# A graph network on one core: six of a basis' sixteen pieces mixed in the bucket stage, and deeper rings of one-hots in the placing stage

## The reference

```python
def rgcn_gate_layer(x, row, col, edge_type, basis, att, gate_w, root, bias):
    w = jnp.einsum('rb,bio->rio', att, basis)      # 30 bases of 512 x 512 mixed into 2 relations
    x_j = x[col]
    msgs = []
    for r in range(2):
        gate = jax.nn.sigmoid(x_j @ gate_w[r, :, 0])
        msgs.append(gate[:, None] * x_j @ w[r])
    msg = jnp.where((edge_type == 0)[:, None], msgs[0], msgs[1])
    return jax.ops.segment_sum(msg, row, num_segments=1250) + x @ root + bias
...
x = _layernorm(x + _L0_gnn_ref(x, edge_index_t, 1250, L0_gnn_W, L0_gnn_b), axis=-1)
...
x = _layernorm(x + _L3_gnn_ref(...), axis=-1)
```

## Time and profile before

| | |
|---|---|
| median of 3 runs | 1955.77 us (1955.05 to 1958.15) |
| profiled execution: time, and span of its instructions | 1963.35 us, 1961.5 us |
| bucket stage, first VectorE instruction to that of the next stage | 138.00 to 182.68 us |
| placing stage, likewise | 182.68 to 314.61 us |
| busy over the span: TensorE, its weight loads, VectorE, ScalarE, GpSimd | 82%, 50%, 59%, 24%, 35% |

### The profile page before, as it was taken

How to read it: one execution, slowest core, us unless ns; L and a number is a source line. 1 busy time by engine, 2 the same in 40 slices (tenths; PEclk the granted TensorE clock), 3 DMA queues, 4 the chain that set the end, 5 groups by cost and what they waited for, 6 DMA issues and landing times. The chain is left out here.

```text
span 1961.5 us, 27790 instructions
## 1 busy us (share of the span) xinstructions
PE 1613.1 (82%) x7565; PEld 984.4 (50%) x7566; DVE 1164.8 (59%) x2302; ACT 471.8 (24%) x884; POOL 684.4 (35%) x605
## 2 busy tenths in 40 slices
PE   6751886777588999998888639988498899999998
PEld 6641553334443555554555425544245545874486
DVE  5678656886356777776477776665773822113222
ACT  4300112433311555554344310000110111001100
POOL 0002834887265776661000247776340010000000
PEclk9999988999679999999989669999799999999999
DMA  0002885001920776673279327777104301430033
GB/s 25 0 0 86 279 294 189 1 1 54 350 85 38 206 206 187 186 176 71 96 282 353 130 76 210 208 211 188 35 1 129 108 0 38 171 134 1 1 133 134
DMA packets 76201, 248.91 MB, mean 127 GB/s; under 512 B 14758, under 2 KB 28439, under 8 KB 68203
## 3 DMA queue, kind: packets, MB, share of 16 engines
q1 hardware_dynamic: 38474, 147.06, 21.0%
q0 software_dynamic: 34592, 96.87, 18.7%
q10 hardware_dynamic: 3072, 4.20, 0.7%
HBM read 215.91 MB, written 32.00 MB: 126 GB/s over the span
## 5 line engine op out<-in xcount | busy, mean ns | idle before, releaser
L645 POOL DMA_INDIRECT tab_slots<-slot_words,slot_address x160 | 220.5, 1378 | 286.4 <-issue 231.0
L1424 PE MATMUL dense_pY<-weights,dense_xT_block 128*128 128x512 f32 x640 | 284.4, 601 | 0.0
L674 POOL DMA_INDIRECT e_rows<-tab_h,idx_h x176 | 174.9, 994 | 297.8 <-POOLq L50 220.1
L1472 PE MATMUL dense_pY<-parts,dense_number 128*128 128x512 f32 x1000 | 238.4, 400 | 6.9 <-DMA dense_number<-tab_edges_to 6.8
L975 POOL DMA_INDIRECT e_rows<-tab_q,idx_q x192 | 182.4, 950 | 98.5 <-issue 39.8
L1472 PEld LDWEIGHTS dense_pY<-parts,dense_number 128*128 128x128 f32 x1000 | 189.3, 190 | 54.7 <-DMA dense_number<-tab_edges_to 8.0
L768 PE MATMUL e_pS<-e_rows,e_onehot_ring 128*128 128x512 f32 x352 | 195.4, 646 | 21.0 <-DVE e_rows L744 18.5
L1424 PEld LDWEIGHTS dense_pY<-weights,dense_xT_block 128*128 128x128 f32 x640 | 121.6, 194 | 143.5 <-issue 143.2
L1048 PE MATMUL e_pS<-e_rows,e_onehot_f 128*128 128x512 f32 x384 | 181.4, 596 | 0.0
L858 PE MATMUL count_pA<-count_onehot_d,count_onehot_s 128*128 128x512 f16 (+1 forms) x576 | 119.6, 355 | 46.7 <-DVE count_onehot_d L836 44.6
L744 DVE TENSOR_TENSOR e_rows<-e_rows,e_pW 128x1024 f32<-128x1024 f32 x88 | 107.3, 1220 | 68.9 <-DMA e_rows<-tab_h,idx_h 68.9
(11 more groups left out here) (312 smaller groups left out, 2459.8 us busy)
## 6 DMA issues: line engine op xcount, KB each, us to landing
basis_piece<-in_L_gnn_basis_pieces SPq DMA_DIRECT2D x32, 2048.0 KB, 8.0
dense_number<-tab_edges_from SPq DMA_DIRECT2D x20, 1280.0 KB, 5.5
tab_edges_from<-counts_turned SPq DMA_DIRECT2D x10, 1280.0 KB
tab_edges_to<-counts_total SPq DMA_DIRECT2D x10, 640.0 KB
dense_number<-tab_edges_to SPq DMA_DIRECT2D x10, 640.0 KB, 4.6
tab_w<-basis_wout ACTq DMA_DIRECT2D x128, 32.0 KB
weights<-tab_w SPq DMA_DIRECT2D x4, 1024.0 KB, 6.6
weights<-in_L_gnn_W_T SPq DMA_DIRECT2D x3, 1024.0 KB
```

The lines of the kernel that those rows point to most:

```text
L645: pool.indirect_dma_start(self.table, bass.IndirectOffsetOnAxis(self.address[:, t:t + 1], 0), self.words[:, t, :], None).then_inc(self.pla ...
L674: pool.indirect_dma_start(self.rows[:, q, s, :], None, self.table, bass.IndirectOffsetOnAxis(self.idx[:, j * 2 + s:j * 2 + s + 1], 0)).the ...
L1424: ins = self.nc.tensor.matmul(self.banks.at(g), self.xt[:, b % 2, c, :], weights[:, c, :], start=c == 0, stop=c == 3)
L1472: ins = self.nc.tensor.matmul(self.banks.at(self.first + b), self.number[:, b % 2, r * NB + k, :], self.parts[r][n][:, k, :], start=k == 0 ...
```

## The change

A `Basis` is now given the range of pieces that it mixes (`first`, `last`), and its number of steps follows from it (two pieces a step). The first basis is made twice: pieces 0 to 5 for the bucket stage and 6 to 15 for the placing stage. `bucket_edges` gets instructions on SyncE (loads) and ScalarE (copies and stores), and on TensorE mixes of half pieces on both sides of the two counting matmuls. In `place_edges` a step is 32 columns instead of 20, a quarter 8 instead of 5; partition one-hots are built four columns at a time in four batches instead of five in two; the ring of slot one-hots has eight places instead of four. The second basis' stage only takes its number of steps from the object, which is 8 as before.

```diff
+WITH_BUCKETS = 6
...
     PIECES = D * D // BCH // BW
-    STEPS = PIECES // 2
...
+        self.first, self.steps = first, (last - first) // 2
...
         def step(i):
             for k in range(2):
                 wait(eng, self.used, (i * 2 + (k - 1)) * 2)
-                eng.dma_start(self.piece[:, k, :], self.pieces[bass.ds((i * 2 + k) * P, P), :]
+                eng.dma_start(self.piece[:, k, :], self.pieces[bass.ds((i * 2 + (k + self.first)) * P, P), :]
                               ).then_inc(self.loaded[k], 16)
-        peeled(eng, self.STEPS, step)
+        peeled(eng, self.steps, step)
...
 def bucket_edges(...)
+        basis.begin(ctx, sem)
         block = ctx.enter_context(nc.Block())
+
+        @block.sync
+        def _(sp):
+            basis.load(sp)
+
+        @block.scalar
+        def _(act):
+            for n in range(basis.steps * 4):
+                basis.store(act, n // 4, n // 2 % 2, n % 2)
+            basis.end_store(act)
...
         @block.tensor
         def _(pe):
+            def mix(first, last):
+                for n in range(first, last):
+                    basis.multiply(pe, n // 4, n // 2 % 2, n % 2)
+
+            basis.start_multiply(pe)
+            mix(0, 4)
             pe.wait_ge(counted, 1)
             nc.tensor.matmul(pC[0:EP, 0, :], C.f("earlier", EP)[:, 0:EP], count[:, :], start=True, stop=True)
             nc.tensor.matmul(pC[:, 1, :], ones[:, :], count[:, :], start=True, stop=True,
                              skip_group_check=True).then_inc(summed, 1)
+            mix(4, basis.steps * 4)
...
 def place_edges(...)
-    RING, STEP = 4, T // Basis.STEPS
+    RING, STEP = 8, T // basis.steps
     QUARTER = STEP // 4
-    TOGETHER = QUARTER
+    TOGETHER, BATCHES = 4, 4
...
-        onp = c1.enter_context(nc.sbuf_tensor(f"{name}_onehot_p", [EP, 2, TOGETHER, P], F32))
+        onp = c1.enter_context(nc.sbuf_tensor(f"{name}_onehot_p", [EP, BATCHES, TOGETHER, P], F32))
...
-                        wait(v, placed, i * STEP + (u - TOGETHER))
+                        wait(v, placed, i * STEP + (u + TOGETHER - BATCHES * TOGETHER))
```

More of the change, by code:

```diff
@@ L172, with __init__ @@
     PIECES = D * D // BCH // BW
-    STEPS = PIECES // 2
-    def __init__(self, nc, name, pieces, mix, wtab):
+    def __init__(self, nc, name, pieces, mix, wtab, first, last):
         self.nc, self.name = nc, name
         self.pieces, self.mix_in, self.dst = pieces, mix, wtab
+        self.first, self.steps = first, (last - first) // 2
     def begin(self, ctx, sem):
@@ L224, in store @@
                 act.dma_start(
-                    self.dst[:, bass.ds((i * 2 + k) * BW, BW)].rearrange("r (s f) -> r s f", s=2)[:, :, q * D:(q + 1) * D],
+                    self.dst[:, bass.ds((i * 2 + (k + self.first)) * BW, BW)].rearrange("r (s f) -> r s f", s=2)[:, :, q * D:(q + 1) * D],
                     self.wout[ROWS * q:ROWS * q + REL * BCH, k, :, :]).then_inc(self.stored[k], 16)
@@ L229, in end_store @@
         for k in range(2):
-            act.wait_ge(self.stored[k], self.STEPS * 64)
+            act.wait_ge(self.stored[k], self.steps * 64)
 def sort_edges(nc, name, C, identb, key, packed, pair_block, block_f, block_turn, block_bank, block_end, pos_p, pos_s, value, address):
@@ L458, in _, with bucket_edges @@
                 peeled(pe, T // GT // 2, step)
-def bucket_edges(nc, name, C, key, rel, packed, pair_block, tile_bucket, tile_bank, bucket_end, pos_p, pos_s, value):
+def bucket_edges(nc, name, C, key, rel, packed, pair_block, tile_bucket, tile_bank, bucket_end, pos_p, pos_s, value, basis):
     with ExitStack() as ctx:
@@ L589, in step @@
                     basis.store(act, i, n // 2, n % 2)
-            peeled(act, Basis.STEPS, step)
+            peeled(act, basis.steps, step)
             basis.end_store(act)
@@ L616, in step @@
                     pe.wait_ge(built, i * STEP + (u + 1))
-                    nc.tensor.matmul(po[:, 0:slots], onp[:, u // TOGETHER % 2, u % TOGETHER, :], ons[:, u % RING, :],
+                    nc.tensor.matmul(po[:, 0:slots], onp[:, u // TOGETHER % BATCHES, u % TOGETHER, :], ons[:, u % RING, :],
                                      start=first and u == 0, stop=last and u == STEP - 1).then_inc(placed, 1)
@@ L1759, in edge_scores @@
         basis.begin(ctx, sem)
-        mixing = lambda i: 1 <= i <= Basis.STEPS if isinstance(i, int) else True
+        mixing = lambda i: 1 <= i <= basis.steps if isinstance(i, int) else True
         block = ctx.enter_context(nc.Block())
@@ L1766, in steps @@
             step(1)
-            with eng.Fori(2, Basis.STEPS + 1) as i:
+            with eng.Fori(2, basis.steps + 1) as i:
                 step(i)
-            for i in range(Basis.STEPS + 1, STEPS):
+            for i in range(basis.steps + 1, STEPS):
                 step(i)
@@ L2094, in gnn @@
         src_block, src_lo, types = (keep(n, [P, SLOTS], F32) for n in ("src_block", "src_lo", "types"))
-        basis = [Basis(nc, f"basis{l}", ins[f"L3_gnn_basis{l + 1}_pieces"], ins[f"L3_gnn_att{l + 1}_mix"],
-                       tab[f"w{l + 1}"]) for l in range(2)]
+        basis = [Basis(nc, f"basis{l}_{first}", ins[f"L3_gnn_basis{l + 1}_pieces"], ins[f"L3_gnn_att{l + 1}_mix"],
+                       tab[f"w{l + 1}"], first, last)
+                 for l, first, last in ((0, 0, WITH_BUCKETS), (0, WITH_BUCKETS, Basis.PIECES), (1, 0, Basis.PIECES))]
         at_top = stage_semaphores(nc, top, "slots")
@@ L2146, in gnn @@
             bucket_edges(nc, "src", C, f(SRC), f(REL1), [(f(DST), 1 << SH1)], pairs["src"][:, :], tile_bucket[:, :],
-                         tile_bank[:, :], bucket_end[:, :], pos_p, pos_s, value)
-            place_edges(nc, "src", C, SRC_SLOTS, pos_p, pos_s, value, packed_src[:, :], basis[0],
+                         tile_bank[:, :], bucket_end[:, :], pos_p, pos_s, value, basis[0])
+            place_edges(nc, "src", C, SRC_SLOTS, pos_p, pos_s, value, packed_src[:, :], basis[1],
                         table)
@@ L2258, in gnn @@
             es, ed = (ctx.enter_context(nc.sbuf_tensor(f"edge_{n}", [P, SLOTS, H], F32)) for n in ("e_src", "e_dst"))
-            edge_scores(nc, "scores", C, identb, est, edt, src_lo, src_block, loc["dst"], pairs["dst"], es, ed, basis[1])
+            edge_scores(nc, "scores", C, identb, est, edt, src_lo, src_block, loc["dst"], pairs["dst"], es, ed, basis[2])
             attention_weights(nc, "att", C, es, ed, factor, loc["dst"][:, :], block_of_pair[:, :],
```

2 lines of the change are left out of this document (1 added, 1 removed).

## The result

The changed kernel takes 1936.69 us (median of 4 runs, 1936.31 to 1937.81), the kernel before 1955.41 us (4 runs beside it). The ratio is 0.9901, with a 95% interval of 0.9888 to 0.9914: faster by 18.7 us. Forecast were 1923 us and a gain of 32.8 us; the sign was right, the size was not, and the time lies 0.7 us outside the range.

What follows compares the result with a forecast made beforehand. Piece loading was taken to pace the placing stage, VectorE alone the bucket stage. Placing gives up some 36.8 us, the bucket stage takes 4.0 back: 32.8 us off the 1955.77 median makes 1923 us, range 1917 to 1936.

Steps and rivals of the forecast that it cites:

- the first mixes and the delay of VectorE: Bucket stage: first mix at 147.2; four mixes ahead of the counting matmuls make VectorE 4.0 us later.
- the low bound of 2.4: Bucket stage: VectorE only 2.4 us later if the mixes run at full rate.
- TensorE in the placing stage: Placing stage: units of 3.91 us, 3 us of waits for loads; TensorE ends at S + 90.0.
- The scatters start their last: Placing stage: GpSimd's scatters are through at S + 86.3, before TensorE, so they do not end the stage.
- scatters of 1.9 us that end the stage: Placing stage: scatters sharing the DMA engines take 1.9 instead of 1.53 us; gain 20 us (1936); chance 0.04.
- I carry the same 32.8 us over: Whole kernel: the 32.8 us gained in the profiled 1963.35 us also come off the median of 1955.77 us.
- the sum of the bounds: Whole kernel: gain between 37.4 us (1918) and 20.4 us (1935, mixing ends the bucket stage plus two low-clock spells).
- the two spells: Rival, placing stage: waits bring the clock down twice, costing 11.3 us; gain 24.5 us, 1931 us; chance 0.14.
- The mixing did not end the bucket stage: Rival, bucket stage: slow loads let mixing end it, placing starts 5.8 us later, 1929 us; chance 0.10.
- TensorE did not stay low: Rival, placing stage: TensorE at the low clock throughout, 38 us slower than before (1994); chance 0.03.
- The rings: Placing stage: rings of eight let VectorE run ahead while TensorE mixes, needing 3.68 us a unit, under 3.91.

Runs made afterwards that it cites:

- 28 early scatters: Changed kernel with 28 of the 160 scatters in the bucket stage, 44 while placing, 88 while counting, none while storing: 1930.5 us, ratio 0.9867.
- deep rings alone: Kernel before with a slot ring of 10 and four partition batches of five, all sixteen pieces in the placing stage: 1957.12 us, ratio 0.9997.
- the run with two half pieces first: Changed kernel with 20 scatters in the bucket stage and two half pieces instead of four mixed ahead of the counting matmuls: 1920.73 us, ratio 0.9814.

## Why the prediction was wrong, step by step

**Nearly right, and priced too high: the first mixes and the delay of VectorE.** The first mix came at 146.04 (147.2 forecast), two half pieces with the durations of the low rate (3.64 us, though the granted clock of their window reads 1.00), and the second piece at 150.82 (150.6). Its two halves went at the full rate (1.93 us for both), so VectorE had its sums 15.56 us after the stage's start against 13.33 before: 2.2 us later, a little under the low bound of 2.4, not 4.0: the low rate, which I gave to three of the four mixes, lasted for two. Those two cost nothing, since TensorE waited 1.14 us for the second piece behind them. VectorE ended the stage and covered the rest of the mixing, so placing started at 185.06 instead of 186.7.

**Right in kind, 5 us too long: TensorE in the placing stage.** No load is waited for after the first, where 3 us were put down for such waits, and the clock stays up (granted 1.00 from 202 to 270 us). Units take 3.79 us at first (3.91 forecast) and 3.99 later, in step with VectorE: its half unit is 0.60 + 1.39 us, so that there VectorE, which was forecast to need 3.68 us for two of them, sets the pace. TensorE's last mix ends at 270.05, 85.0 us after the stage's start; forecast were 90.

**Wrong: "The scatters start their last at 85.12 us after the stage's first instruction and take 1.2 us, so GpSimd is through at S + 86.3 and not last."** This is the step that failed. It took the scatters' pace of 1.53 us as their own. Of the 56, 35 took 1.99 us, and GpSimd was through at 287.31, S + 102.3 (S, the stage's first VectorE instruction, is 185.06 here). The next stage started 3.06 us later: S + 105.3 instead of S + 95.1, 10.2 us lost. Against TensorE's own end, S + 85.0 and the tail of 5.1 us, it is 15.2 us; the 5 us that the forecast gave TensorE too much hide the rest. What the 3.06 us consist of is not shown. In the three other runs in which scatters end a stage (old rings, all sixteen pieces, 28 early scatters) it was 3.04 to 3.26 us, where VectorE ended the bucket stage 0.9 us.

The cause, as the runs showed it: a scatter that starts while VectorE is in a partition one-hot, a TENSOR_TENSOR with both inputs in SBUF, is held up by the rest of it, 0.51 us. With 1.48 us for the scatter itself this makes 1.99, and VectorE's half unit is 1.99 too, so that each scatter begins where the last one did, 0.04 us into a partition one-hot. It is a trap for more than this one period: 0.04, 0.51 and 1.48 put the next start 2.03 us after that of the one-hot, so with any half unit from 1.48 to 2.03 it falls into the next one and is held up again. The half unit of 2.145 in the run with slot numbers in PSUM is over that, and there three of four scatters went free. Before, VectorE waited for TensorE 45.9 us, its one-hots came unevenly, and the scatters mostly fell between them. Five of the 56 started in the first 0.6 us of one, and they show the same rule: the later in it, the less they were held up, from 1.76 us for a start 0.11 us into the one-hot to 1.31 us for one 0.56 us into it. Of the other 51 the median is 1.18 us. Two of the five, all engines, kernel before:

```profile
195.26 0.81 DVE L601 TENSOR_TENSOR src_onehot_p<-const_table,pos_partition 125x640 f32<-125x640 f32 x1
195.58 1.53 POOL L645 DMA_INDIRECT tab_slots<-slot_words,slot_address  x1 [0.30 <-issue]
...
256.55 0.82 DVE L601 TENSOR_TENSOR src_onehot_p<-const_table,pos_partition 125x640 f32<-125x640 f32 x1
256.66 1.76 POOL L645 DMA_INDIRECT tab_slots<-slot_words,slot_address  x1 [0.30 <-issue]
```

The wait that the change removed was GpSimd's free road. In the changed kernel itself this shows at 194.85 to 199.30: VectorE's one wait, 3.3 us until 196.81, breaks the step, and four scatters in a row take 1.17 to 1.18 us. The 2.03 is worked out from the rows; one half unit on either side of it was run.

The Trainium skill (SBUF — State Buffer, SBUF: two separate sides) has a rule that fits: VectorE and GpSimd share a pair of ports as an exclusive lock held for a whole instruction, and VectorE takes it, among others, with two SBUF inputs against a GpSimd operation that reads SBUF. The trace agrees: 1.69 us with two SBUF inputs, 1.18 with one in PSUM. Which instruction holds a scatter up, and for how long, the runs show; that it does so through these ports they don't show by themselves.

**Its place among the rivals.** The prediction had scatters of 1.9 us that end the stage, at 1936 us, with a chance of 0.04. The size was close (1.82 us a scatter on the mean), but the reason given, sharing of the DMA engines, was not right (the run with all pieces in the bucket stage), and that its time is within 1 us of the measured one is in part luck: it puts the next stage at S + 108.2, 294.9 us, which is 4.5 too late, and counts its gain from a profile that was long (below). With the right reason it should have been the forecast, as VectorE was said to run "near" without pause.

**Wrong too: "I carry the same 32.8 us over."** Part of the profiled placing stage of before was that execution's own: it took 131.93 us there (clock 0.92), 124.06 in the second profile (0.98), and 126.64 (0.94) with deep rings alone, whose time is the same and whose profile lies at its median. So some 5 to 8 us of the 32.8 were not there to be gained in a median execution. The account with the second profile: 32.8 forecast, 1.6 more from a cheaper bucket stage, less 10.2 for the scatters and 7.9 for the profile, is 16.3; behind the stage 1.4 are lost: 14.9. That is, but for rounding and the starts of the stages, the 15.2 us between the two spans (1949.8 and 1934.6). The medians differ by 18.7, 3.5 more: the second profile's execution (1951.56 us) was 3.8 us under the median of its own runs (1955.32), the changed kernel's 0.3 under its own.

**Wrong in the sum of the bounds.** By its own prices the low bound is 32.8 less 5.8 for the bucket stage and 8.3 for the two spells, 18.7 us and 1937 us, not 20.4 and 1935. That would have taken the measured time in, but by two events that did not come.

**The rivals that did not come.** The mixing did not end the bucket stage (it does once VectorE is served earlier, in the run with two half pieces first). No spell of low clock came between units, and TensorE did not stay low.

**The rings.** The prediction let rings of eight carry VectorE ahead; with the old rings the time is the same, and the 2.0 us that TensorE ends later with them stay hidden behind the scatters. What depth is worth once the scatters run free was not tried.

## What to carry to other kernels

The pace of an engine off the path is not its own as long as another engine's waits leave it room: when a change removes those waits, price the hidden engine's work again under an unbroken partner, above all GpSimd's scatters beside VectorE instructions that read two tiles of SBUF. If the two periods can lock, put one input in PSUM or move some of the work. And before a gain read from one profile is carried over to a median, compare the length of just that stage in a second profile of the same kernel.

## What was not expected of the hardware

- A scatter on GpSimd takes 1.48 us from start to start alone, 1.99 beside unbroken partition one-hots with both inputs in SBUF, and up to 6.8 us when it starts during a scan of 3200 columns; a TENSOR_REDUCE of 5.58 us doesn't hold it up.
- VectorE pays as well: four slot one-hots are busy for 1.24 to 1.25 us in the kernel before once GpSimd is through (278.69 to 304.46), and for 1.47 in step with the scatters. From their start to the next instruction they take 1.39 us in step, and 1.17 to 1.56 beside free scatters (partition numbers in PSUM). Which moment of a scatter holds them up was not tried.
- Reading one input of the partition one-hot from PSUM costs VectorE nothing (0.60 us from start to start in both), while the slot one-hots went from 0.35 to 0.385 us.
- Scatters beside the storing stretch's transfers are not free: 12 more cost 5.0 us, 16 fewer gave 4.7 back.
